# Scores of a windowed attention in 64x64 tiles, each query half with the 192 keys that it may see

## The chip, the cores and the metric

The kernel runs on one core of a Trainium2 chip. The metric is the device time of one execution in microseconds (us). TensorE (PE in the profile) multiplies, PEld is the loading of its stationary operand, VectorE (DVE), ScalarE (ACT) and GpSimd (POOL) do the rest, and SyncE (SP) issues the DMAs.

## The reference

The model is an adaLN block on `x` of 2 x 2048 x 256 in float32. Its first half is three layers of causal linear attention with a feed-forward part; its second half is two layers of windowed attention, 8 heads of 64, window 128, with a gated feed-forward part. The change touches the scores of the second half alone:

```python
def local_attention(q, k, v):
    b, h, n, d = q.shape
    w = n // WINDOW
    bq = q.reshape(b, h, w, WINDOW, d) * QK_SCALE
    bk = k.reshape(b, h, w, WINDOW, d)
    ...
    bk, bv = (look_around(bk), look_around(bv))   # block before and own block
    sim = jnp.einsum('bhwid,bhwjd->bhwij', bq, bk)
    mask = (i < j) | (i > j + WINDOW) | (j == -1)
    sim = jnp.where(mask, -jnp.finfo(sim.dtype).max, sim)
    attn = jax.nn.softmax(sim, axis=-1)
```

A query at place r of its block sees the keys r to 127 of the block before and the keys 0 to r of its own: 129 of 256. Of the 256 columns of a score row, queries 0 to 63 never need the last 64, and queries 64 to 127 never the first 64.

## The kernel before

The second half works on 64 units of 128 tokens (2 layers, 2 batch rows, 16 blocks each); unit u is a block, and units with u % 16 == 0 have no block before them. The heads stand as four head pairs: in `QT` and `KT` the 128 partitions are two heads of 64 features, and a head pair's 128 tokens are 128 columns. `KT` keeps two units' keys, the present one in slot u % 2 and the one before in the other slot, so that in odd units the block before comes first in it, and in even ones the present block.

The order of every engine's work is written out by hand: a long list of calls such as `scores_tile(u, hf)`, `turn_weights(u, g)`, `mix(u, hf)`, with semaphores (`e.wait_ge(*...at(u))`, `.then_inc(...)`) between engines. Within that list, feed-forward work of other tokens (`up`, `gate`, `down` in fp32r as three products of high and low parts) is laid between the steps of attention.

For each unit and each half `hf` of the head pairs: `scores_tile` writes the scores of two head pairs into PSUM banks 3 and 4 (`PS[:, 3 + par, ...]`, one bank for each head of the pair); DVE `largest` adds the mask `MSK` and takes row maxima over the PSUM tile, in place; ACT `exps` writes `PR`; PE `turn_weights` transposes `PR` back into PSUM; `copy_p` (half on ACT, half on DVE) writes `PT`; PE `mix` multiplies with the values `VV`. ACT's `copy_k` (line 2206) and `copy_q` (line 2213) fill `KT` and `QT` after PE has transposed keys and queries (lines 927 and 936). Products with plain fp32 operands appear in the trace as two weight loads and two matmul records each (two passes), fp32r products and transposes as one.

In `scores_tile` the stationary operand is `QT[r, c]`, 64 features by 128 queries, the moving one is `KT[r, :, c]`, 256 keys as two pieces of 128. The two heads of a pair stand in different partition halves and go to different row halves of the array. All matmuls are recorded under the helper `mm` at line 276; `PS<-KT,QT` names the scores, `PS<-PT,VV` the products with the values.

Of the kernel before, what the change touches and what calls it, by code (L numbers as in the profile page):

```python
# [41 lines left out]
def build(nc, ctx, ins, out):  # L42
# [252 lines left out]
    def wt(nm, a, n):  # L295
        o = REG[nm] + a
        if nm == "w1":
            return W1H[:, o:o + n], W1L[:, o:o + n]
        if nm == "w2":
            return W2H[:, o:o + n], W2L[:, o:o + n]  # L300
        return WQH[:, o:o + n], WQL[:, o:o + n]

    def va(o, n):
# [116 lines left out]
    def _(e):  # L420
# [518 lines left out]
        def scores_tile(u, hf):  # L939
            if not 0 <= u < NU:  # L940
                return
            first, cur = u % 16 == 0, u % 2
            e.wait_ge(*b_qt.at(u))
            e.wait_ge(*b_kt.at(u))
            if hf:
                e.wait_ge(*b_pt[0].at(u))
                e.wait_ge(*g_pt[0].at(u))
            elif u >= 1:
                e.wait_ge(*b_rs.at(u - 1))
                e.wait_ge(*g_pt[1].at(u - 1))  # L950
            else:
                e.wait_ge(*d_h.at(23, 1))
                e.wait_ge(*g_x.at(2))
            for i in range(2):
                for par in range(2):
                    r, c = slice(64 * par, 64 * par + 64), slice(128 * (2 * hf + i), 128 * (2 * hf + i) + 128)
                    if first:
                        m = mm(e, PS[:, 3 + par, 256 * i + 128 * cur:256 * i + 128 * cur + 128], QT[r, c], KT[r, cur, c], i == 0)
                    else:
                        m = mm(e, PS[:, 3 + par, 256 * i:256 * i + 256].rearrange("p (b n) -> p b n", b=2), QT[r, c], KT[r, :, c], i == 0)  # L960
            m.then_inc(*f_sc[hf].up(u))

        def blocks(u):
            return (u % 2,) if u % 16 == 0 else (0, 1)

# [11 lines left out]
        def mix(u, hf):  # L977
# [10 lines left out]
            for i in range(2):  # L988
                hp = 2 * hf + i
                for b in blocks(u):  # L990
                    for par in range(2):
                        start = hf == 0 and i == 0 and b == blocks(u)[0]
                        v = u if b == u % 2 else u - 1
                        m = mm(e, PS[64 * par:64 * par + 64, 2, 128 * hp:128 * hp + 128], VV[:, v % 3, 64 * (2 * hp + par):64 * (2 * hp + par) + 64],
# [877 lines left out]
    def _(e):  # L1872
# [328 lines left out]
        def copy_k(u):  # L2201
            if 0 <= u < NU:
                e.wait_ge(*f_tk.at(u))
                if u >= 1:
                    e.wait_ge(*f_sc[1].at(u - 1))
                e.copy(KT[:, u % 2, :], PS[:, 7, :]).then_inc(*b_kt.up(u))

# [7 lines left out]
        def exps(u, g):  # L2215
            if not 0 <= u < NU:
                return
            hf, par, S = g // 2, g % 2, SM[:, u % 4, :]
            lo, hi = (128 * (u % 2), 128 * (u % 2) + 128) if u % 16 == 0 else (0, 256)
            e.wait_ge(*g_bi[g].at(u))  # L2220
# [10 lines left out]
        def copy_p(u, hf):  # L2231
            if not 0 <= u < NU:
                return
            lo, hi = (128 * (u % 2), 128 * (u % 2) + 128) if u % 16 == 0 else (0, 256)
            e.wait_ge(*f_wg[2 * hf].at(u))
# [739 lines left out]
    def _(e):  # L2975
# [580 lines left out]
        def largest(u, g):  # L3556
            if not 0 <= u < NU:
                return
            hf, par, S = g // 2, g % 2, SM[:, u % 4, :]
            lo, hi = (128 * (u % 2), 128 * (u % 2) + 128) if u % 16 == 0 else (0, 256)  # L3560
            z = 128 if u % 16 == 0 else (0 if u % 2 else 128)
            if u == 0:
                e.wait_ge(*t_ms.at())
            e.wait_ge(*f_sc[hf].at(u))
            for i in range(2):
                o = PS[:, 3 + par, 256 * i + lo:256 * i + hi]
                t = e.tensor_tensor_reduce(o, o, MSK[:, z:z + hi - lo], 1.0, NEG, ALU.add, ALU.max, S[:, 32 + 2 * g + i:33 + 2 * g + i])  # L3567
            t.then_inc(*g_tt[g].up(u))
# [5 lines left out]
        def copy_p(u, hf):  # L3574
            if not 0 <= u < NU:
                return
            lo, hi = (128 * (u % 2), 128 * (u % 2) + 128) if u % 16 == 0 else (0, 256)
            e.wait_ge(*f_wg[2 * hf + 1].at(u))
# [1957 lines left out]
```

## Time and profile before

| | |
|---|---|
| time, median of 3 runs | 2609.28 us (2607.87 to 2610.86) |
| profiled execution | 2610.22 us, its span 2608.4 us |
| busy in the span | PE 97%, DVE 82%, POOL 55%, ACT 54% |
| chain that ended last | PE 87%, DVE 6%, issue 3%, ACT 2%, POOL 1% |
| mean granted TensorE clock | 0.989 of full speed |
| scores of the second half | 128 calls, 1024 matmul records, 142.8 us busy |

The 1.8 us between the span and the execution's time lie around the program. Busy time of PE is the union of its records; since the ends of matmuls are modelled and overlap their successors, what a group costs is read from its start to the start of the next group.

### The profile page before, as it was taken

What the parts mean: (1) busy time and instruction counts of PE and PEld (TensorE: products, weight loads), DVE (VectorE), ACT (ScalarE), POOL (GpSimd) and SP (SyncE); (2) the same over time, 40 slices, a digit from 0 to 9 for tenths busy, and PEclk for the clock granted to TensorE, in tenths of its full rate; (3) what the DMA queues carried; (4) which work ended last, traced back from release to release, by engine and by line L of the source; (5) the groups of instructions that cost most, each with busy time, mean ns of one, the idle gap of its engine ahead of it and who ended that gap; (6) DMA issues with size and microseconds to landing.
All of it is one profiled execution on the core that took longest, in us unless ns stands there. A gap on an engine that the chain in (4) does not pass through costs nothing.

```text
span 2608.4 us, 65564 instructions
## 1 busy us (share of the span) xinstructions
PE 2523.3 (97%) x23520; PEld 2094.4 (80%) x23520; DVE 2143.9 (82%) x5253; ACT 1405.0 (54%) x2945; POOL 1427.1 (55%) x1406
## 2 busy tenths in 40 slices
PE   6899999999999999999998999999999999999998
PEld 4688888888888888887776788888888888888877
DVE  5798888887787788898999887888898887888875
ACT  3343344334433443344256777777776777777761
POOL 2253444443444355455576666666676766776664
PEclk8899999999999999999999999999999999999999
DMA  3100000010000010000112000000111100110001
GB/s 91 38 18 10 18 2 18 14 36 2 2 2 14 14 42 10 18 26 26 49 38 66 21 17 19 12 16 17 32 32 36 33 29 23 32 32 28 27 29 49
DMA packets 79088, 67.44 MB, mean 26 GB/s; under 512 B 15896, under 2 KB 73368, under 8 KB 78776
## 3 DMA queue, kind: packets, MB, share of 16 engines
q1 hardware_dynamic: 78776, 63.25, 8.1%
q8 instruction: 199, 3.26, 0.5%
q14 instruction: 113, 0.93, 0.1%
HBM read 49.18 MB, written 12.58 MB: 24 GB/s over the span
## 4 chain that ended last, share of the span: by engine, by line
PE 87%; DVE 6%; issue 3%; ACT 2%; POOL 1%; DMA 0%; SPq 0%; DVEq 0%; ACTq 0%; POOLq 0%
PE PS L276 76%; PE PS L974 4%; PE PS L936 1%; PE PS L1004 1%; PE PS L927 1%; PE PS L488 1%; PE PS L498 1%; PE PS L431 1%; PE PS L885 1%; DVE U L3159 1%; DVE PS L3567 1%; PE PS L1034 1%; DVE Z L2997 0%; ACT PR L2227 0%; DVE X L3005 0%
## 5 line engine op out<-in xcount | busy, mean ns | idle before, releaser
L2227 ACT ACTIVATE PR<-PS,SM 128x256 f32<-128x256 f32 (+1 forms) x512 | 280.7, 561 | 136.5 <-DVE SM L3572 135.9
L1913 ACT ACTIVATE FB<-PS,BC 128x512 f32<-128x512 f32 x192 | 133.5, 695 | 322.1 <-PE PS L276 174.9
L3159 DVE TENSOR_TENSOR U<-PS,CST 128x512 f32<-128x512 f32 x384 | 238.0, 681 | 37.5 <-PE PS L276 37.4
L4597 POOL TENSOR_TENSOR RL<-FB,RH 128x512 fp32r<-128x512 f32 x96 | 125.7, 1310 | 219.6 <-DVE RH L3136 219.6
L4819 POOL TENSOR_TENSOR SM<-SM,COL 128x8 f32<-128x8 f32 x128 | 224.6, 1755 | 10.7
L276 PE MATMUL PS<-W2H,RH 128*128 128x256 f32 x768 | 226.1, 294 | 2.2 <-POOL RL L4597 2.2
L3567 DVE CUSTOM_DVE_ANT_0 PS<-PS,MSK 128x256 f32<-128x256 f32 (+1 forms) x512 | 202.5, 436 | 30.5 <-PE PS L276 29.5
L276 PE MATMUL PS<-W2H,RL 128*128 128x256 f32 x768 | 215.8, 281 | 0.0
L276 PE MATMUL PS<-W2L,RH 128*128 128x256 f32 x768 | 215.7, 281 | 0.0
L4609 POOL TENSOR_TENSOR SBD<-SBD,TMP 128x256 f32<-128x256 f32 x84 | 64.8, 772 | 197.0 <-DVE TMP L3151 197.0
L276 PEld LDWEIGHTS PS<-W2H,RH 128*128 128x128 f32 x768 | 145.0, 189 | 25.0 <-issue 20.4
L276 PE MATMUL PS<-X1H,W1H 128*128 128x512 f32 x384 | 160.9, 419 | 3.5 <-ACT FB L1913 2.4
L276 PE MATMUL PS<-VAH,XBH 128*128 128x512 f32 x384 | 162.9, 424 | 1.0 <-ACT SQ L2176 0.6
L276 PE MATMUL PS<-X1L,W1H 128*128 128x512 f32 x384 | 151.7, 395 | 0.0
L276 PE MATMUL PS<-VAH,XBL 128*128 128x512 f32 x384 | 151.3, 394 | 0.0
L276 PE MATMUL PS<-VAL,XBH 128*128 128x512 f32 x384 | 151.2, 394 | 0.0
L276 PE MATMUL PS<-X1H,W1L 128*128 128x512 f32 x384 | 151.0, 393 | 0.0
L276 PE MATMUL PS<-KT,QT 64*128 64x256 f32 (+1 forms) x1024 | 142.8, 397 | 8.4 <-ACT PT L2240 5.8
L276 PEld LDWEIGHTS PS<-W2L,RH 128*128 128x128 f32 x768 | 145.2, 189 | 2.4
L276 PEld LDWEIGHTS PS<-W2H,RL 128*128 128x128 f32 x768 | 145.1, 189 | 0.0
L974 PE MATMUL PS<-CST,PR 128*128 128x128 f32 x992 | 137.4, 274 | 7.7 <-ACT PR L2227 7.6
L4832 POOL TENSOR_TENSOR OTL<-OO,OTH 128x512 fp32r<-128x512 f32 x64 | 83.0, 1296 | 103.8 <-ACT OTH L2263 103.6
(268 smaller groups left out, 8467.4 us busy)
## 6 DMA issues: line engine op xcount, KB each, us to landing
PX<-in_L_attn_x SPq DMA_DIRECT2D x16, 512.0 KB, 3.9
TB<-in_k_rot SPq DMA_DIRECT2D x64, 128.0 KB, 2.1
SG<-in_L_attn_W SPq DMA_DIRECT2D x24, 256.0 KB, 2.8
xp_scratch<-PX SPq DMA_DIRECT2D x8, 512.0 KB, 2.9
xs_scratch<-X SPq DMA_DIRECT2D x64, 64.0 KB, 1.5
ZS<-xs_scratch SPq DMA_DIRECT2D x16, 256.0 KB, 2.8
GG<-xp_scratch SPq DMA_DIRECT2D x7, 512.0 KB, 3.7
out<-GG SPq DMA_DIRECT2D x7, 512.0 KB, 2.9
```

The source lines that it names most:

```text
L276: return e.matmul(o, l, r, start=start, stop=True, skip_group_check=True)
L431: t = e.transpose(PS[:, 2 + k, 128 * j:128 * j + 128], X[:, 4 * c + j, 128 * k:128 * k + 128], IDN)
L488: t = e.transpose(PS[:, i, D * j + 128 * m:D * j + 128 * m + 128], FK[:, m, 128 * (2 * i + j):128 * (2 * i + j) + 128], IDN)
L974: m = e.transpose(PS[:, 3 + par, a:a + 128], PR[:, par, a:a + 128], IDN)
L1913: e.activation(FB[:, hb % 2, :], PS[:, 5, :], ACT.Relu, bias=BC[:, l % 2, 4 + hb:5 + hb]).then_inc(*a_re.up(n, hb))
L2227: t = e.activation(PR[:, par, 256 * i + lo:256 * i + hi], PS[:, 3 + par, 256 * i + lo:256 * i + hi], ACT.Exp, bias=S[:, 40 + 2 * g + i:41 ...
L3159: e.tensor_tensor(heads(U[:, u % 6, :], 4), heads(PS[:, g, :], 4), bcast(CM, 4), ALU.mult).then_inc(*d_mk.up(n, u))
L3567: t = e.tensor_tensor_reduce(o, o, MSK[:, z:z + hi - lo], 1.0, NEG, ALU.add, ALU.max, S[:, 32 + 2 * g + i:33 + 2 * g + i])
L4597: e.tensor_tensor(RL[:, r, :], FB[:, 0, :], RH[:, r, :].bitcast(F), ALU.subtract).then_inc(*p_rl.up(n, hb))
L4609: e.tensor_tensor(SBD[:, (tile + 1) % 2, :, :], SBD[:, tile % 2, :, :], TMP[:, :, :], ALU.add).then_inc(*p_sd.up(n, j))
L4819: e.tensor_tensor(o, a, MHALF.broadcast_to([128, 8]), ALU.pow).then_inc(*h_rs[i].up(u))
L4832: e.tensor_tensor(OTL[:, :], OO[:, :], OTH[:, :].bitcast(F), ALU.subtract).then_inc(*h_ol.up(u))
```

## The change

Each head of a head pair's scores is cut into two query halves. The stationary operand is now 64 features by 64 queries, and the four combinations of head and query half use four quarters of the array: rows by head, columns by query half. The first query half gets the keys 0 to 191 of the sequence (block before, own block), the second the keys 64 to 255. In PSUM the block before now always stands first. `KT` is laid out anew: for each head pair slot 0 and slot 1 stand beside each other, so that the 192 keys are contiguous where slot 0 holds the block before (odd units). In even units the two pieces stand in the wrong order for that, and each tile takes two matmuls of 128 and 64 or of 64 and 128 keys. A call of `scores_tile` thus issues 4 matmuls of 256 columns before; now 8 of 192 columns in the 32 odd units, 16 of 64 or 128 columns in 28 even units, and in the 4 first units of a row 8 of 64 or 128 columns where there were 4 of 128. The 64 columns that a query half does not write keep what PSUM held, and the mask puts them out.

```diff
+    def keys_of(b):
+        return KT.rearrange("p x (h b n) -> p (x h) b n", h=2, b=2)[:, :, b, :]
...
             for i in range(2):
+                c = 128 * (2 * hf + i)
                 for par in range(2):
-                    r, c = slice(64 * par, 64 * par + 64), slice(128 * (2 * hf + i), 128 * (2 * hf + i) + 128)
-                    if first:
-                        m = mm(e, PS[:, 3 + par, 256 * i + 128 * cur:256 * i + 128 * cur + 128], QT[r, c], KT[r, cur, c], i == 0)
-                    else:
-                        m = mm(e, PS[:, 3 + par, 256 * i:256 * i + 256].rearrange("p (b n) -> p b n", b=2), QT[r, c], KT[r, :, c], i == 0)
+                    for half in range(2):
+                        r, p, a = slice(64 * par, 64 * par + 64), slice(64 * half, 64 * half + 64), 256 * i
+                        Q = QT[r, c + 64 * half:c + 64 * half + 64]
+                        if first or cur == 0:
+                            before, here = 128 if half == 0 else 64, 64 if half == 0 else 128
+                            if not first:
+                                mm(e, PS[p, 3 + par, a + 128 - before:a + 128], Q, keys_of(1 - cur)[r, 2 * hf + i, 128 - before:128], i == 0)
+                            m = mm(e, PS[p, 3 + par, a + 128:a + 128 + here], Q, keys_of(cur)[r, 2 * hf + i, 0:here], i == 0 and first)
+                        else:
+                            m = mm(e, PS[p, 3 + par, a + 64 * half:a + 64 * half + 192], Q, KT[r, hf, 256 * i + 64 * half:256 * i + 64 * half + 192], i == 0)
             m.then_inc(*f_sc[hf].up(u))

         def blocks(u):
-            return (u % 2,) if u % 16 == 0 else (0, 1)
+            return (1,) if u % 16 == 0 else (0, 1)
...
-                        v = u if b == u % 2 else u - 1
+                        v = u - 1 + b
...
-                e.copy(KT[:, u % 2, :], PS[:, 7, :]).then_inc(*b_kt.up(u))
+                e.copy(keys_of(u % 2), PS[:, 7, :].rearrange("p (h n) -> p h n", h=4)).then_inc(*b_kt.up(u))
...
-            z = 128 if u % 16 == 0 else (0 if u % 2 else 128)
...
-                t = e.tensor_tensor_reduce(o, o, MSK[:, z:z + hi - lo], 1.0, NEG, ALU.add, ALU.max, S[:, 32 + 2 * g + i:33 + 2 * g + i])
+                t = e.tensor_tensor_reduce(o, o, MSK[:, lo:hi], 1.0, NEG, ALU.add, ALU.max, S[:, 32 + 2 * g + i:33 + 2 * g + i])
```

`exps`, `copy_p` and `largest` use `lo, hi = 128 if u % 16 == 0 else 0, 256`; their sizes stay.

PE, an odd unit in the second half, scores between projections and a product of the feed-forward part. Before (a row is line, operation, output and operands, shape of the output, how many in a row):

```order
L276 MATMUL PS<-VAH,XBH 128x512
L276 MATMUL PS<-VAL,XBH 128x512
L276 MATMUL PS<-VAH,XBL 128x512
L276 MATMUL PS<-KT,QT 128x256 x4
L276 MATMUL PS<-VBH,RH 128x256 x4
```

After, the same place:

```order
L276 MATMUL PS<-VAH,XBH 128x512
L276 MATMUL PS<-VAL,XBH 128x512
L276 MATMUL PS<-VAH,XBL 128x512
L276 MATMUL PS<-KT,QT 64x192 x8
L276 MATMUL PS<-VBH,RH 128x256 x4
```

Four matmuls have become eight narrower ones, and nothing around them has moved.

PE, an even unit that is not the first of its row, scores between the products with the values and transposes of the feed-forward part. Before:

```order
L1004 MATMUL PS<-CST,RX 128x128 x4
L276 MATMUL PS<-PT,VV 64x128 x8
L276 MATMUL PS<-KT,QT 128x256 x4
L1034 MATMUL PS<-CST,ZS 128x128 x8
L885 MATMUL PS<-CST,X 128x128 x2
```

After:

```order
L1013 MATMUL PS<-CST,RX 128x128 x4
L276 MATMUL PS<-PT,VV 64x128 x8
L276 MATMUL PS<-KT,QT 64x128
L276 MATMUL PS<-KT,QT 64x64 x2
L276 MATMUL PS<-KT,QT 64x128 x2
L276 MATMUL PS<-KT,QT 64x64 x2
L276 MATMUL PS<-KT,QT 64x128 x2
L276 MATMUL PS<-KT,QT 64x64 x2
L276 MATMUL PS<-KT,QT 64x128 x2
L276 MATMUL PS<-KT,QT 64x64 x2
L276 MATMUL PS<-KT,QT 64x128
L1043 MATMUL PS<-CST,ZS 128x128 x8
```

Here four matmuls have become sixteen, and two that follow each other go to the same quarter of the array: 128 and 64 columns to the first, 64 and 128 to the second, and so on.

## Rows read from the trace of the kernel before

**Rows 1.** The page: busy us, share of the span, number of instructions.

```profile
PE 2523.3 (97%) x23520; PEld 2094.4 (80%) x23520; DVE 2143.9 (82%) x5253; ACT 1405.0 (54%) x2945; POOL 1427.1 (55%) x1406
```

**Rows 2.** Busy time by stretch: us, busy (instructions), PEclk, DMA share, GB/s.

```profile
1306.00:1400.00 94.00, 83.96 (x585) 67.48 (x583) 90.98 (x254) 52.19 (x130) 68.20 (x68) 0.98 0.19 53
1400.00:2500.00 1100.00, 1087.50 (x7941) 903.76 (x7942) 910.95 (x2592) 812.35 (x1857) 741.34 (x762) 1.00 0.09 27
2500.00:2608.00 108.00, 93.89 (x628) 79.78 (x626) 68.93 (x161) 37.72 (x83) 48.69 (x43) 0.95 0.12 37
```

**Rows 3.** Waits of PE, 1306 to 2608 us: total, times, longest.

```profile
PE PS L974 <- ACT PR L2227: 7.6, 12, 1.6
PE PS L276 <- ACT PT L2240: 5.8, 7, 0.9
...
PE PS L276 <- DVE PT L3583: 2.5, 3, 1.3
```

**Rows 4.** PE's groups: busy us, mean ns, idle before.

```profile
L276 PE MATMUL PS<-KT,QT 64*128 64x256 f32 x960 | 137.1, 404 | 7.6 <-ACT PT L2240 5.1 <-DVE PT L3583 2.5
...
L276 PE MATMUL PS<-KT,QT 64*128 64x128 f32 x64 | 5.7, 297 | 0.7 <-ACT PT L2240 0.7
```

**Rows 5.** PE's timeline in two units: start us, length us, instruction, number.

```profile
1956.93 1.13 PE L276 MATMUL PS<-KT,QT 64*128 64x256 f32 x8
1957.99 1.09 PE L276 MATMUL PS<-PT,VV 128*64 128x128 f32 x16
1959.02 0.66 PE L936 MATMUL PS<-CST,QS 128*128 128x128 f32 x4
...
1618.97 0.71 PE L276 MATMUL PS<-KT,QT 64*128 64x128 f32 x8
1619.61 0.66 PE L1034 MATMUL PS<-CST,ZS 128*128 128x128 f32 x4
```

**Rows 6.** The same scores cut off at 1957.20 and at 1957.40 us.

```profile
1956.93 0.49 PE L276 MATMUL PS<-KT,QT 64*128 64x256 f32 x2
...
1956.93 0.70 PE L276 MATMUL PS<-KT,QT 64*128 64x256 f32 x4
```

**Rows 7.** Weight loads (PEld), 1306 to 2608 us: busy us, mean ns, idle before.

```profile
L276 PEld LDWEIGHTS PS<-PT,VV 128*64 128x64 f32 x1984 | 107.5, 138 | 31.9 <-issue 31.3
L276 PEld LDWEIGHTS PS<-KT,QT 64*128 64x128 f32 x1024 | 88.1, 187 | 40.2 <-issue 31.8
```

**Rows 8.** PE's timeline in the first half, four column groups.

```profile
928.51 0.33 PE L276 MATMUL PS<-VP,KS 128*32 128x32 f32 x16
928.65 1.06 PE L276 MATMUL PS<-U,VP 128*32 128x128 f32 x32
929.64 1.15 PE L276 MATMUL PS<-FQ,FK 32*128 32x256 f32 x16
```

**Rows 9.** PE's timeline in the first half, sixteen 32x32 tiles, two passes each.

```profile
914.23 0.62 PE L276 MATMUL PS<-U,OM 32*32 32x512 f32 x3
914.25 0.61 PE L276 MATMUL PS<-KS,OM 32*32 32x512 f32 x1
...
914.33 0.61 PE L276 MATMUL PS<-KS,OM 32*32 32x512 f32 x1
914.68 0.60 PE L276 MATMUL PS<-U,OM 32*32 32x512 f32 x3
...
915.11 0.82 PE L276 MATMUL PS<-U,CST 32*32 32x512 f32 x3
```

**Rows 10.** Groups of ACT and DVE, 1306 to 2608 us: busy us, mean ns, idle before.

```profile
L2240 ACT COPY PT<-PS 128x512 f32<-128x512 f32 x120 | 70.3, 586 | 39.7 <-PE PS L974 39.2
...
L2206 ACT COPY KT<-PS 128x512 f32<-128x512 f32 x64 | 37.5, 586 | 43.3 <-PE PS L927 41.5 <-PE PS L276 1.8
...
L3567 DVE CUSTOM_DVE_ANT_0 PS<-PS,MSK 128x256 f32<-128x256 f32 x480 | 193.8, 444 | 29.2 <-PE PS L276 28.4
```

More of the change, by code:

```diff
@@ L2218, in exps @@
             hf, par, S = g // 2, g % 2, SM[:, u % 4, :]
-            lo, hi = (128 * (u % 2), 128 * (u % 2) + 128) if u % 16 == 0 else (0, 256)
+            lo, hi = 128 if u % 16 == 0 else 0, 256
             e.wait_ge(*g_bi[g].at(u))
@@ L2233, in copy_p @@
                 return
-            lo, hi = (128 * (u % 2), 128 * (u % 2) + 128) if u % 16 == 0 else (0, 256)
+            lo, hi = 128 if u % 16 == 0 else 0, 256
             e.wait_ge(*f_wg[2 * hf].at(u))
@@ L3559, in largest @@
             hf, par, S = g // 2, g % 2, SM[:, u % 4, :]
-            lo, hi = (128 * (u % 2), 128 * (u % 2) + 128) if u % 16 == 0 else (0, 256)
-            z = 128 if u % 16 == 0 else (0 if u % 2 else 128)
+            lo, hi = 128 if u % 16 == 0 else 0, 256
             if u == 0:
@@ L3576, in copy_p @@
                 return
-            lo, hi = (128 * (u % 2), 128 * (u % 2) + 128) if u % 16 == 0 else (0, 256)
+            lo, hi = 128 if u % 16 == 0 else 0, 256
             e.wait_ge(*f_wg[2 * hf + 1].at(u))
```

## The prediction

> **What bounds the kernel now.** I read the busy shares first: PE is busy 97% of the span, every other engine less [rows 1]. Then the second half by stretch, since the change lies only there: from 1400 to 2500 us PE is busy 1087.5 of 1100 us at the full clock, with DVE at 83%, ACT at 74% and POOL at 67%; in the first 94 us DVE is the fuller one (91 of 94), and the last 108 us are an emptying tail [rows 2]. Third the waits: PE's longest kinds of wait in the half are 7.6 us behind the exponentials and 5.8 and 2.5 us behind the copies of the weights [rows 3]. So between 1400 and 2500 us the time is what PE's list of matmuls costs, and a microsecond taken from it is nearly a microsecond of the kernel. The scores are 1024 matmul records, of which 960 have 256 columns [rows 4]; what they cost has to be read from start to start.
>
> **How such a matmul is priced.** A call of `scores_tile` with 256 columns takes 1957.99 − 1956.93 = 1.06 us, one with 128 columns 1619.61 − 1618.97 = 0.64 us [rows 5]. Each is eight records, but two run at a time: 0.27 us after the start only two are on record, at 1957.40 four [rows 6]. So it is four turns of two, and 128 more columns cost 0.42/4 = 0.105 us a turn, or 0.82 ns a column. What remains is fixed: 0.64 − 0.42 = 0.22 us for the first weights, which nothing hides, and for running empty before the array is set up for another shape. A load of 64 stationary columns is recorded 49 ns shorter than one of 128 (138 against 187 ns) [rows 7]; the products with the values fit that, eight turns of 128 columns in 1.03 us, 0.19 us of it fixed [rows 5].
>
> **Do four quarters run at once?** The scores before use two row halves, the products with the values two column halves, and no row shows both together at 64x64. The nearest rows do more: with sixteen 32x32 tiles all first passes start between 914.23 and 914.33 us and the second ones from 914.68, 0.45 us later for 512 columns at a price of 0.42 [rows 9], so rows and columns combine at full rate, about 7 ns from one start to the next. With four column groups over the same rows, 16 passes of 32 columns, each with weights of its own, take 928.65 − 928.51 = 0.14 us, 0.035 a turn of four, where streaming alone is 0.026 [rows 8]. So weights for one column group load while another works, and a turn costs some 5 to 9 ns beyond its columns. The Trainium skill says otherwise ("TensorE: Matmul & The Clock Gate", Part 3, The mechanism): weight loads overlap running matmuls only where the row groups differ. By it each call would show four loads more, some 0.2 us, and most of the gain would go; the rows on four column groups contradict it.
>
> **Odd units (32 units, 64 calls).** Eight matmuls of 192 columns on four quarters are again four turns, of 192 columns: 0.64 + 4 × 64 × 0.82 ns = 0.85, less 0.05 for the shorter first weights, plus two more starts of 7 ns: 0.81 us for 1.06. 64 × 0.25 = 16.0 us. This has one answer.
>
> **First units (4 units, 8 calls).** 64 and 128 columns on the two halves: the 128 set the time, as before, with shorter first weights. 0.64 to 0.60 us, 8 × 0.04 = 0.3 us.
>
> **Even units (28 units, 56 calls).** This is the disputed part. Sixteen matmuls; each quarter gets 128 + 64 or 64 + 128 columns a head pair, 192 again, but in eight passes instead of four. If the quarters work independently, the call is an odd unit's plus four passes a quarter at 5 to 9 ns: 0.81 + 0.03 = 0.84 us, and 56 × 0.22 = 12.3 us are saved. But now two successive matmuls go to the same quarter, and if the second has to wait at the head of the queue, the other quarters behind it starve. No row of before shows two successive matmuls for one quarter with matmuls for others behind them; all its tiled groups change the tile with every matmul. For independence speaks that a later matmul does pass an earlier one's second pass: the second head's first pass is on record 0.3 us before the first head's second one [rows 6], and sixteen matmuls are open at once, each with its second pass to come, when the next starts [rows 9]. The queue is therefore no strict line of passes. Whether it is a strict line of matmuls it doesn't say. I take independence, since whatever holds back sixteen second passes has room for one matmul that waits for its quarter; the other end is priced as a rival.
>
> **The rest.** ACT's copy into `KT` now writes four pieces of 128 at a stride; it is 586 ns now, the same as the copy into `PT` [rows 10]; nothing in its size changes and I cost it at nothing. If it grew by 0.1 us, 64 × 0.1 us on an engine at 74% would hide under PE. DVE's `largest` and the exponentials keep their shapes [rows 10]; the unwritten 64 columns are read as before. No wait and no DMA is added, and no queue is passed.
>
> **Sum.** 16.0 + 0.3 + 12.3 = 28.6 us less on PE. Not all arrives: the first 94 us, where DVE is fuller than PE, and the tail hold about 200 of 1302 us, so roughly a tenth of the calls, and what waits there are stays. I take 2 us off: 26.6. Against the profiled execution (2610.2 us) that is 2583.6, against the median of the runs (2609.3, 0.9 lower) 2582.7, say 2583. If the other engines followed worse than that, 5 us more would be lost; if the even calls cost as little as the odd ones, 1.7 us would be won: this case alone holds 2576 to 2591.
>
> **Rivals.**
> 1. *The waiting matmul blocks the queue until its quarter can take its weights* (0.18, slower). Per head pair the four quarters then begin one after the other, each new one only when the one before has begun its second pass: load 0.05 + first pass 0.107, load 0.05 + 0.055, and the same again, 0.52 to 0.57 us with the starts. Two head pairs 1.14, then the last quarter's last 0.055 + 2 × 0.107, and 0.09 to run empty: 1.5 us for 1.06. 56 × 0.44 = 24.6 us lost against 16.3 won: 2617. It decides on the even units alone: beyond 1.35 us a call the change loses.
> 2. *Matmuls start strictly in program order* (0.13, slower). Then the second matmul of a quarter starts only after the first has ended, and the next quarter with it: 0.218 + 0.11 + 0.218 + 0.11 = 0.66 us a head pair, twice, plus 0.218 at the end and 0.14 fixed, 1.67 us a call; 56 × 0.61 = 34 lost, net 18 slower: 2627. The rows neither show nor exclude it. This is also a rule of the Trainium skill, in the place named above: matmuls start and end in program order, a strict FIFO.
> 3. *PE gets ahead and then waits for others* (0.10, of which 0.08 faster and 0.02 the same). After the scores come mask and maxima on DVE (444 ns each, four a call) [rows 10] and the exponentials before PE may transpose. The work between stays the same, so the distance is kept, and PE's waits of that kind are only 16 us [rows 3]; against it speaks too that DVE has 17% free. If half of the gain went so: 2596.
> 4. *The four quarters don't overlap* (0.02, slower): two at a time, eight turns of 192 columns, 1.4 us a call and 2650; the rows on sixteen tiles speak against it.
>
> **How the numbers follow.** Forecast 0.57, rivals 0.18, 0.13, 0.10, 0.02. Faster by over 0.2% (5 us, about what a measurement of this kernel can tell from no change): 0.57 + 0.08 = 0.65; same 0.02; slower 0.33. The cases lie on both sides. The likeliest one's own range is 2576 to 2591; to hold 8 in 10 the range has to reach over rival 3 and most of rival 1: 2576 to 2622, which leaves out rivals 2 and 4 and edges.
>
> **What would show it.** Per call, start to next start: odd 0.81 us (all cases but rival 4), first 0.60, even 0.84 (forecast), 1.5 (rival 1), 1.67 (rival 2). In an even call cut off 0.1 us after its start, four matmuls should be under way; under rivals 1 and 2 it is one or two. The waits of PE behind `PR` and `PT` should stay near 16 us; under rival 3 they grow by 10 or more. I am wrong outright if the odd calls don't shrink by 0.25 us, or if ACT's copy into `KT` grows enough to be waited for.

## The result, and the profile after

Four runs of each kernel give a median of 2594.05 us after (2589.8 to 2596.7) for 2608.66 us before: a ratio of 0.9941 with an interval of 0.9924 to 0.9958. In a second series, of five rounds, it was 2589.34 for 2605.40 us, 0.9936 (0.9924 to 0.9949). By the medians the change takes 14.6 and 16.1 us off; the forecast was 26.6. The sign and the range hold, and more than ten microseconds of the forecast are missing. One execution of a kernel below (rotated, `turn_tile` and `high_x` later) took 8366 us, for a reason that no trace shows, and is left out of its median.

The page of after (answers to [rows 1]; chain by engine; groups as on the page):

```profile
PE 2499.2 (97%) x25440; PEld 2085.6 (81%) x25440; DVE 2147.5 (83%) x5253; ACT 1404.7 (54%) x2945; POOL 1428.8 (55%) x1406
...
PE 86%; DVE 7%; issue 4%; ACT 2%; POOL 1%; DMA 1%; SPq 0%; DVEq 0%; ACTq 0%; POOLq 0%
```

The same stretches as in [rows 2] (length, PE, PEld, DVE, ACT, POOL busy, granted clock, DMA share, GB/s):

```profile
1306.00:1400.00 94.00, 81.63 (x729) 66.85 (x727) 89.81 (x265) 54.63 (x140) 69.03 (x72) 0.97 0.21 58
1400.00:2500.00 1100.00, 1086.08 (x9806) 913.65 (x9808) 926.62 (x2613) 820.60 (x1874) 749.01 (x769) 1.00 0.09 26
2500.00:2588.00 88.00, 72.51 (x503) 61.84 (x497) 51.97 (x116) 24.73 (x52) 35.37 (x28) 0.95 0.14 45
```

PE is as full as before, with the clock at its full level between 1400 and 2500 us; DVE goes from 911 to 927 us in the middle stretch, because the same work now stands in less time. The waits of PE in the second half are those of [rows 3], nearly unchanged:

```profile
PE PS L276 <- ACT PT L2249: 6.7, 8, 1.0
PE PS L983 <- ACT PR L2236: 6.6, 12, 1.5
...
PE PS L276 <- DVE PT L3591: 1.5, 2, 1.3
...
PE PS L888 <- DVE OO L3610: 0.9, 4, 0.3
```

One kind is new, the last: L888 is `turn_tile`, the transposes of `X` (line 885 before), and `OO` is what DVE makes of the products with the values. It looks like nothing, 0.9 us in four places. It will turn out to be most of what is missing. ACT's copy into `KT` and DVE's maxima have kept their lengths [rows 10]; only the idle time ahead of the maxima has shrunk from 29.2 to 13.7 us:

```profile
L2215 ACT COPY KT<-PS 128x512 f32<-128x512 f32 x63 | 36.9, 586 | 37.9 <-PE PS L930 36.4 <-PE PS L276 1.5
...
L3575 DVE CUSTOM_DVE_ANT_0 PS<-PS,MSK 128x256 f32<-128x256 f32 x480 | 193.7, 444 | 13.7 <-PE PS L276 10.9
```

Now the calls themselves, on PE's timeline of after: a first unit's, an even unit's and an odd unit's, each with the group that follows [rows 5]. A group bears the name of the form it begins with, so the 32 records of the even call are those of 128 and of 64 columns.

```profile
1608.85 0.67 PE L276 MATMUL PS<-KT,QT 64*64 64x64 f32 x16
1609.45 0.33 PE L1043 MATMUL PS<-CST,ZS 128*128 128x128 f32 x1
...
1960.40 0.96 PE L276 MATMUL PS<-KT,QT 64*64 64x128 f32 x32
1961.30 0.33 PE L276 MATMUL PS<-PT,VV 128*64 128x128 f32 x2
...
1979.29 0.88 PE L276 MATMUL PS<-KT,QT 64*64 64x192 f32 x16
1980.10 0.39 PE L276 MATMUL PS<-VBH,RH 128*128 128x256 f32 x1
```

The odd call takes 0.81 us, as forecast; the first one 0.60, as forecast; the even one 0.90 us (0.895 in the median), where 0.84 was forecast. The records inside the even call say which picture of the queue is right. Windows that begin with the call and look at the scores alone (length, PE busy, records, clock, DMA):

```profile
1960.40:1960.45 0.05, 0.04 (x4) 1.00 0.00 0
1960.40:1960.60 0.20, 0.20 (x9) 1.00 0.00 0
```

Within 0.05 us four matmuls are under way, the first ones of the four quarters, 13 to 14 ns apart. The trace gives their lengths as 128, 64, 128 and 64 columns, where the program's first four are 128, 64, 64 and 128: these are matmuls 1, 3, 5 and 7. Each but the first stands in the program behind the second matmul of the quarter before, which has to wait; they have passed it. That refutes rivals 1 and 2 for this order.

**A better measure than the span.** The kernel's first half, which no edit touches, varies between executions: the first scores of the second half start at 1308.7 us in the profiled run of before, at 1301.8 in that of after, and between 1300.6 and 1308.7 in all fourteen profiled runs, those of the experiments included. Of the 20.4 us between the two spans, 7 lie ahead of the first changed instruction. I therefore read each trace from the first scores of unit 4 to the first scores of unit 62. Two executions of before give 1116.6 and 1116.9 us for this stretch of 58 units, two of after 1103.6 and 1103.6. The change is worth 13.1 us there; by the forecast it should be 58 × 0.25 + 6 × 0.04 + 52 × 0.22 = 26.2.

Where the 13.1 us are, by what PE issues, each group from its start to the next start: scores −18.1, transposes of `X` in `turn_tile` +2.3, transposes of `PR` +0.8, products with the values +0.5, all else +1.4.

### The profile page after: what moved, and what is told of

Same layout as the page of the kernel before. It is cut to its first block, busy times and chain, and to the rows that moved or that the text cites. A ratio compares the mean times of both kernels' runs of the same rounds, so it can differ in the third digit from the quotient of the medians.

```text
span 2588.0 us, 69404 instructions
## 1 busy us (share of the span) xinstructions
PE 2499.2 (97%) x25440; PEld 2085.6 (81%) x25440; DVE 2147.5 (83%) x5253; ACT 1404.7 (54%) x2945; POOL 1428.8 (55%) x1406
## 4 chain that ended last, share of the span: by engine, by line
PE 86%; DVE 7%; issue 4%; ACT 2%; POOL 1%; DMA 1%; SPq 0%; DVEq 0%; ACTq 0%; POOLq 0%
PE PS L276 75%; PE PS L983 4%; PE PS L939 1%; PE PS L930 1%; PE PS L1013 1%; PE PS L501 1%; PE PS L491 1%; PE PS L434 1%; PE PS L888 1%; PE PS L1043 1%; DVE U L3168 0%; DVE PS L3575 0%; DVE Z L3006 0%; DVE ST L2995 0%; DVE X L3014 0%
## 5 line engine op out<-in xcount | busy, mean ns | idle before, releaser
L276 PE MATMUL PS<-HTH,VBH 128*128 128x512 f32 x330 | 138.6, 420 | 1.0 <-ACT G L2301 0.8
L276 PE MATMUL PS<-PT,VV 128*64 128x128 f32 x1984 | 139.1, 282 | 0.6 <-DVE XBL L3535 0.6
```

Source lines behind the costliest of these rows:

```text
L276: return e.matmul(o, l, r, start=start, stop=True, skip_group_check=True)
```

## The experiments

A ratio is to before in the same series, on the same chip, with its 95% interval; the series ran on three chips, with medians of before between 2605.4 and 2607.0 us, so the ratios are to be compared, not the medians. "The stretch" is units 4 to 61 as just defined, from one trace of each kernel; "against before" is its difference from 1116.6 us.

| kernel | median us | ratio | stretch us | against before |
|---|---|---|---|---|
| before (second execution) | 2602.3, one run | | 1116.9 | +0.3 |
| the change, again | 2589.3 | 0.9936 (0.9924 to 0.9949) | 1103.6 | −13.0 |
| quarters in odd units alone | 2598.7 | 0.9969 (0.9955 to 0.9982) | 1110.3 | −6.3 |
| rotated quarters | 2584.2 | 0.9919 (0.9906 to 0.9932) | 1100.6 | −16.0 |
| one quarter's matmuls in a row | 2646.4 | 1.0151 (1.0136 to 1.0166) | 1155.9 | +39.2 |
| three key slots | 2592.0 | 0.9950 (0.9938 to 0.9962) | 1105.1 | −11.6 |
| `turn_tile` later | 2597.6 | 0.9968 (0.9956 to 0.9980) | 1114.8 | −1.8 |
| rotated, `turn_tile` and `high_x` later | 2586.2 | 0.9931 (0.9918 to 0.9944) | 1102.0 | −14.7 |
| three slots, the same two later | 2590.9 | 0.9946 (0.9934 to 0.9958) | 1104.7 | −11.9 |
| before with a short `OO` | 2599.3 | 0.9973 (0.9961 to 0.9984) | 1112.7 | −4.0 |
| the change with a short `OO` | 2574.9 | 0.9882 (0.9865 to 0.9898) | 1089.8 | −26.8 |
| rotated, `reduce` behind the maxima | 2583.1 | 0.9911 (0.9898 to 0.9925) | 1100.7 | −15.9 |

### The change and the kernel before, once more

> The changed kernel once more, for a second profile and more times. The first profile showed odd calls of 0.81 us, even ones of 0.895, first ones of 0.598, and the transposes behind 45 of the calls (turn_tile, on PSUM bank 2) starting 0.955 us after the scores' start whatever the scores took, behind DVE's product OO. Theory 1 (the price list of PE less that new floor): 16.1 + 9.5 + 0.4 us saved on calls, 5.2 us given back at the floor, so 20.8 us below the kernel before: 2588 in the median, and the floor at 0.955 again. Theory 2 (something varies from run to run and takes more in most runs): the median stays near 2594, and a profile of such a run shows waits that the first one did not have.

> The kernel before once more, for a second profile. In the profiles so far the first scores start between 1300.6 and 1308.7 us, though nothing ahead of them differs. Theory 1 (the first half varies from execution to execution, and only the distance from the first scores to the end may be compared between profiles): the first scores may start anywhere from 1300 to 1309 us, and from there to the end it is 1299.7 us again, within 2. Theory 2 (the change speeds up the first half too, by where its instructions lie): the first scores start near 1308.7 us again.

They repeat the stretch to 0.3 us and the ratio to 0.0005, while the first scores start 6.5 us apart in the two of before and 4.3 in the two of after. Both pairs suggest that differences of a microsecond in the stretch can be trusted; in the span they can't. The calls and the 0.955 us are those of the first profile, but the 20.8 us that theory 1 worked out from them are not reached: 16.1 by the medians. From the first scores to the end before takes 1298.3 us for 1299.7, as its theory 1 had it.

### Quarters in the odd units alone

```diff
                     if first:
...
+                        m = mm(e, PS[:, 3 + par, a + 128 * cur:a + 128 * cur + 128], QT[r, c:c + 128], keys_of(cur)[r, 2 * hf + i, :], i == 0)
+                    elif cur == 0:
+                        m = mm(e, PS[:, 3 + par, a:a + 256], QT[r, c:c + 128], KT[r, hf, a:a + 256], i == 0)
                     else:
...
+                        for half in range(2):
+                            m = mm(e, PS[64 * half:64 * half + 64, 3 + par, a + 64 * half:a + 64 * half + 192], QT[r, c + 64 * half:c + 64 * half + 64],
+                                   KT[r, hf, a + 64 * half:a + 64 * half + 192], i == 0)
```

> The kernel before with quarters in the odd units alone; even and first units keep 64x128 tiles and all their keys, with the keys laid out anew. Theory 1 (the prices add): 64 odd calls of 0.81 instead of 1.064 save 16.1 us, of which 29 calls in front of turn_tile give 0.144 each back, so 12 us below the kernel before, 2597, and the even units' part of the change is worth the other 8.5. Theory 2 (the list is not what binds): odd alone already gives all of the 14.6 us that the medians show.

The calls are 0.811 us in odd and 1.065 in even units, so a call's price doesn't depend on the other units' form. But 58 odd calls at −0.254 us are 14.7, and the stretch gives 6.3; the scores themselves show only −9.25. Theory 1 had 12 us for the kernel, theory 2 all of 14.6; the medians give 6.7, and neither holds. More than half of what the odd calls save doesn't arrive. So the loss is not a matter of the even units' sixteen matmuls.

### The second matmul of a quarter moved behind the other quarters

```diff
+                for piece in range(2 if cur == 0 and not first else 1):
+                    for par in range(2):
+                        for half in range(2):
...
+                            elif cur == 0 and piece == half:
+                                m = mm(e, PS[p, 3 + par, a + 128 - before:a + 128], Q, keys_of(1 - cur)[r, 2 * hf + i, 128 - before:128], i == 0 and piece == 0)
+                            elif cur == 0:
+                                m = mm(e, PS[p, 3 + par, a + 128:a + 128 + here], Q, keys_of(cur)[r, 2 * hf + i, 0:here], i == 0 and piece == 0)
```

In even units every head pair now issues its 128 columns on all four quarters and then its 64 on all four.

> The changed kernel with the even units' sixteen matmuls in another order: the four quarters in turn, first all pieces of 128 keys, then all of 64, so that no two successive matmuls go to the same quarter. Theory 1 (two successive matmuls for one quarter cost the 0.055 us that an even call has above my 0.84): even calls fall from 0.895 to 0.84 us; those 16 in front of turn_tile win nothing because of the floor at 0.955, the other 40 win 0.055 each, 2.2 us less than the changed kernel. Theory 2 (the passes of 64 columns cost it, in any order): even calls stay at 0.89 and the time too. If a queue of whole matmuls had been blocked in the changed kernel, its even calls would have been 1.5 us, which the profile already excludes.

The same even call in this kernel:

```profile
1959.57 0.90 PE L276 MATMUL PS<-KT,QT 64*64 64x128 f32 x32
1960.40 0.33 PE L276 MATMUL PS<-PT,VV 128*64 128x128 f32 x2
```

0.83 us (0.828 in the median) for 0.895, with the same matmuls; the first four start 7 ns apart instead of 13, and the turns of the four quarters stay in step, where in the change two quarters begin with 64 columns and two with 128 and their turns fall out of step. Fourteen of the stretch's 52 even calls are held at 0.955 us in both kernels, for a reason given below, and win nothing; the other 38 × 0.067 make 2.5 us. The scores alone show 2.3, the stretch 3.0 and the medians 5.2. This is the forecast's 0.84, found in another order of the same instructions. How much of the 0.067 us comes from the passing and how much from the uneven turns, this run doesn't tell apart.

### All matmuls of one quarter behind each other

```diff
-            for i in range(2):
-                c = 128 * (2 * hf + i)
-                for par in range(2):
-                    for half in range(2):
+            for par in range(2):
+                for half in range(2):
+                    for i in range(2):
+                        c = 128 * (2 * hf + i)
```

Odd units then have two matmuls for a quarter in a row, even ones four.

> The changed kernel with the same matmuls in the worst order for a queue: all those of one quarter of the array behind each other (two in odd units, four in even ones), then the next quarter's. Theory 1 (each quarter takes its own matmuls out of the queue, whatever stands in front for another quarter): odd calls stay near 0.81, at most 0.87, even ones near 0.90 and below 1.0. Theory 2 (at most one matmul per quarter may be passed by others, which the changed kernel's order never exceeded): odd calls near 0.85, but even ones above 1.3, since the third matmul for a quarter holds up the other three quarters.

Even call, and windows from its start on (scores alone):

```profile
1993.72 2.05 PE L276 MATMUL PS<-KT,QT 64*64 64x128 f32 x32
1995.70 0.33 PE L276 MATMUL PS<-PT,VV 128*64 128x128 f32 x2
```

```profile
1993.72:1993.77 0.05, 0.05 (x1) 1.00 0.00 0
1993.72:1994.10 0.38, 0.38 (x4) 1.00 0.00 0
1993.72:1994.13 0.41, 0.41 (x6) 1.00 0.00 0
```

The odd call takes only 0.83 us for 0.81: the second matmul of a quarter waits, and the other quarters pass it. The even call takes 1.98 us, more than either rival had for the change. At first one record is under way where the change has four; for 0.38 us only four passes start, those of the first quarter's first two matmuls. Then, at 0.384 us, its third starts, and 5 ns later (0.389) the second quarter's first. That is what a queue would do that holds back one waiting matmul for each quarter and stops at the next: the third could step aside only when the second had started, the fourth only when the third had. Of the first eight matmuls of a call in the change one waits for each quarter, four in all, and none of them stops another. That the queue is built so is inferred from the starts in these two orders; no row shows it directly. I had taken "whatever holds back sixteen second passes has room for one matmul that waits"; it has, and for one only.

The Trainium skill says of this ("TensorE: Matmul & The Clock Gate", Part 3, The mechanism) that matmuls keep program order at both ends, a strict FIFO. The windows of the change contradict it: four records within 0.05 us, of matmuls 1, 3, 5 and 7 of the call. What an order that stops the queue costs is this run's: 52 even calls × 1.085 us are 56.4 more than the change, and the stretch is 52.3 longer.

### Three key slots, so that even units too take 192 columns at once

`KT` gets a third slot, block before, own, and a second copy of the even units' keys, made by ACT; the even units then issue the odd ones' eight matmuls. Room for it comes from letting `RX` be `RS`, so that ACT's copy into `RX` now waits for `OO` too (the last line).

```diff
-                            if not first:
-                                mm(e, PS[p, 3 + par, a + 128 - before:a + 128], Q, keys_of(1 - cur)[r, 2 * hf + i, 128 - before:128], i == 0)
-                            m = mm(e, PS[p, 3 + par, a + 128:a + 128 + here], Q, keys_of(cur)[r, 2 * hf + i, 0:here], i == 0 and first)
...
+                            m = mm(e, PS[p, 3 + par, a + 64 * half:a + 64 * half + 192], Q, key_row(2 * hf + i)[r, z:z + 192], i == 0)
...
+        def twin_k(u):
+            if 0 <= u < NU and u % 2 == 0:
+                e.wait_ge(*b_kt.at(u))
+                e.copy(keys_of(0), keys_of(2)).then_inc(*b_kd.up(u))
...
+                    e.wait_ge(*g_om.at(u - 1))
```

> The changed kernel with a third slot of keys: an even unit's keys go to slot 2, behind the odd unit's in slot 1, and ACT copies them once more into slot 0 for the next unit (64 partitions' pairs as before, 128x512, ahead of the first exponentials); so even units too issue eight matmuls of 192 keys. To make room, the sums' two buffers became one. Theory 1 (an even call then costs what an odd one does, 0.81): 40 calls win 0.084 each over the changed kernel, 3.4 us, the 16 in front of turn_tile nothing, and ACT's 32 further copies of 0.59 us hide in its waits for DVE; about 2586 where the changed kernel is 2589. Theory 2 (the copies delay the exponentials): PE waits more for PR and the time is like the changed kernel's or above it.

The even call falls to 0.811 us, and the kernel is no faster than the change: stretch 1105.1 for 1103.6. The scores are 3.0 us shorter than in the change, the transposes of `PR` 2.6 us longer: ACT has a copy more ahead of the exponentials, and PE waits a little longer for those, 2.9 us in the stretch for 1.9. The waits of the second half, 7.6 us for 6.6 in the change:

```profile
PE PS L989 <- ACT PR L2247: 7.6, 14, 1.5
```

How much of the loss comes from the copies and how much from the shared buffer and its wait, this run doesn't tell apart. Against the rotated order, which needs no copy, there is nothing to gain here.

### Who holds the first half's calls

Of the two calls of a unit only the second (`hf` 1) shows its full gain. The first is followed by `turn_tile`, and there the gain is cut. PE and DVE in before, first call of an odd unit:

```profile
1984.39 1.13 PE L276 MATMUL PS<-KT,QT 64*128 64x256 f32 x8
1984.48 0.69 DVE L3602 TENSOR_TENSOR OO<-PS,RS 128x512 f32<-128x512 f32 x1 [1.62 <-PE PS L276]
...
1985.45 0.44 PE L885 MATMUL PS<-CST,X 128*128 128x128 f32 x2
...
1985.66 0.47 PE L276 MATMUL PS<-VAH,XBH 128*128 128x512 f32 x1
```

The same place in after:

```profile
1969.87 0.88 PE L276 MATMUL PS<-KT,QT 64*64 64x192 f32 x16
1969.99 0.69 DVE L3610 TENSOR_TENSOR OO<-PS,RS 128x512 f32<-128x512 f32 x1 [1.56 <-PE PS L276]
...
1970.83 0.41 PE L888 MATMUL PS<-CST,X 128*128 128x128 f32 x2
...
1971.17 0.47 PE L276 MATMUL PS<-VAH,XBH 128*128 128x512 f32 x1
```

`turn_tile` writes into PSUM bank 2, where the products with the values stand, and first waits until DVE has read them for `OO` (`g_om`, line 884 of after). `OO` starts about 0.1 us after the scores, when the products with the values have ended, and takes 0.69 us. In after it ends at 1970.68, and the transposes start 0.15 us later, at 1970.83: 0.955 us after the scores, which themselves could have given way after 0.811. In before the same wait would have let them go after 0.955 us as well, and the scores took 1.065: a margin of 0.11 us, of which the tables of waits show nothing, and a saving of 0.25 us used it up. In 37 of the 42 first calls of the stretch that `turn_tile` follows, the transposes start 0.95 to 0.96 us after the scores, whether the scores cost 0.811 or 0.895; in before it is 1.065. (Sixteen of its 58 first calls have something else behind them; ten of these are even units' and show their 0.895.) With a few longer ones that makes 5.7 us, 23.8 at the calls' own prices less the 18.1 read.

The trace also has the sequencer's own records. It passes the wait for `OO` at 1970.72, 0.11 us before the transposes, and the three waits behind it at 1970.85, 1970.96 and 1971.06. In before the same four pass at 1985.21, .34, .44 and .55, and the transposes start 0.24 us after the first. Over all 60 places that distance is 0.22 us in the median in before and 0.107 in after. So the next group starts 0.34 us after the transposes where it was 0.21 (medians of the 42: 0.34 and 0.23), since the waits behind `OO`'s are worked off one by one, some 0.11 us each; that makes the 2.3 us on the transposes. The profile puts 0.9 us down to `OO`, since it counts gaps between PE's records, and the modelled ends leave almost none.

Two kinds of experiment test that: another order on PE, and a shorter `OO`.

### `turn_tile` one entry later

```diff
             scores_tile(u + 1, 0)
+            partner(q, 1)
             turn_tile(u + 4)
-            partner(q, 1)
```

and so in every unit where something can stand between.

> The changed kernel with turn_tile put one entry later in PE's list, behind the projection, output product or feed-forward product that followed it, wherever it stood right behind the first scores of a unit. Theory 1 (the transposes wait for PSUM bank 2, that is for DVE's product OO, and this ate 5.2 us of the gain): PE finds the bank free, all odd calls take 0.81 and even ones 0.895 us to the next start, and the kernel is about 5 us below the changed one. Theory 2 (the tiles' copies on ACT come later and hold back the exponentials behind them): PE waits more for PR, and the time is the same or 2 to 5 us longer.

Both calls now show 0.811 and 0.895 us, and the scores save 23.1 us instead of 18.1, as theory 1 says. And the kernel gets slower than the change, by 11.3 us in the stretch, more than either theory had: the transposes of `PR`, counted to the start of the next group, cost 16.0 us more than before, and other products some 5. PE's waits in units 4 to 61 of this kernel:

```profile
PE PS L276 <- ACT GG L2301: 8.1, 11, 0.7
PE PS L983 <- ACT PR L2236: 4.6, 7, 2.1
```

and the second of these kinds in the change, where the first isn't among the waits:

```profile
PE PS L983 <- ACT PR L2236: 1.9, 4, 0.7
```

ACT takes `X` out of PSUM (`high_x`) ahead of the exponentials and, in one unit of four, of `gelu`, which writes `GG`, in a fixed order. A later `turn_tile` makes ACT wait, the exponentials start later (3.71 us after the scores on the average, for 3.49), and `gelu` behind them too. Most of the 16.0 us is PE's wait not for the exponentials but for `gelu`: 11.5 of them lie where a product of the feed-forward part follows the transposes, and eleven of these stand 0.7 us each behind `GG`. The edit took one wait away and made a greater one two steps on, rival 3's kind of mechanism, but from my own edit.

### Rotated, with `turn_tile` and `high_x` later

```diff
             scores_tile(u + 1, 0)
+            partner(q, 1)
             turn_tile(u + 4)
-            partner(q, 1)
...
-        high_x(8)
         high_o(4)
         exps(5, 1)
         copy_v(6)
         exps(5, 0)
+        high_x(8)
```

> The kernel with rotated quarters, with turn_tile one entry later in PE's list, and besides with ACT's copy of the turned tile (high_x) behind the first two exponentials instead of in front of them. With turn_tile alone moved, PE found bank 2 free but waited 16 us more for the exponentials. Theory 1 (those waits came from ACT standing in front of high_x while PE was late with the tile): PE's waits for PR fall back, the scores cost 0.81 and 0.83 us everywhere, and the kernel is 5 to 8 us below the one with rotated quarters alone, some 2578 against 2584. Theory 2 (the tile itself comes too late, for the projections that read it): PE waits in front of the projections instead and the time is no better than with rotated quarters alone.

> Three slots of keys together with turn_tile one entry later and ACT's high_x behind the first two exponentials. Theory 1 (the gains add): all calls 0.81 us, no wait behind OO, about 2 us below the kernel with rotated quarters and those two moves. Theory 2 (ACT, now with 32 copies more and its order changed, comes late): PE's waits for PR and PT rise and the time is above that kernel's.

The expectation says that PE waited 16 us more for the exponentials; as just shown, most of that was for `gelu`. With `high_x` behind the first two exponentials, the scores show their whole gain (−26.2 us), and the surplus on `PR` falls from 16.0 to 7.5 us: the waits for `GG` are gone, so that half of it was indeed ACT's order. It is still no better than rotation alone (1102.0 for 1100.6 us), and with three slots likewise 1104.7. PE's waits behind `PR`, in units 4 to 61, have grown threefold against the change:

```profile
PE PS L986 <- ACT PR L2239: 5.7, 16, 1.5
```

The time is what theory 2 had, but the waits are for `PR` and not in front of the projections. What is taken from one wait is found at the next; that the chain scores, maxima, exponentials, transposes has no slack left in these units is my reading of it, which these runs don't prove.

### A short `OO` in both kernels

```diff
-            e.tensor_tensor(OO[:, :], PS[:, 2, :], RS[:, :], ALU.mult).then_inc(*g_om.up(u))
+            w = 512 if u == 0 else 64
+            e.tensor_tensor(OO[:, 0:w], PS[:, 2, 0:w], RS[:, 0:w], ALU.mult).then_inc(*g_om.up(u))
```

From unit 1 on both kernels leave out seven eighths of this product, 0.23 us on DVE instead of 0.69. All else is issued as before, so the pair measures the change with `OO` off the path.

> The kernel before with the product OO cut to 64 of its 512 columns after the first unit (the output is then not the reference's), so that DVE's 0.69 us between the products with the values and the masks becomes about 0.15. It is the partner of the changed kernel with the same cut. In the kernel before PE hardly waits for DVE there, so both theories expect little: the same, or up to 5 us faster.

> The changed kernel with the product OO cut to 64 of its 512 columns after the first unit (the output is then not the reference's). Theory 1 (the gain that is missing is held by OO: the transposes of turn_tile wait for it, and PE's sequencer stands in front of that wait instead of working off the next ones): the transposes start 0.81 and 0.895 us after the scores, and this kernel lies 22 to 26 us below the kernel before with the same cut, where the full kernels lie 15 to 17 apart. Theory 2 (OO is only where PE happens to wait; the chain through masks and exponentials is what holds): the difference stays at 15 to 18 us and the waits move to the exponentials PR.

The change with a short `OO`, first call of an odd unit:

```profile
1963.02 0.88 PE L276 MATMUL PS<-KT,QT 64*64 64x192 f32 x16
1963.14 0.23 DVE L3611 TENSOR_TENSOR OO<-PS,RS 128x64 f32<-128x64 f32 x1 [1.58 <-PE PS L276]
...
1963.83 0.44 PE L888 MATMUL PS<-CST,X 128*128 128x128 f32 x2
...
1964.02 0.48 PE L276 MATMUL PS<-VAH,XBH 128*128 128x512 f32 x1
```

The transposes follow after 0.81 us and the next group 0.19 us after them. Between the two kernels with a short `OO` the stretch differs by 22.9 us, the medians by 24.4; 23.8 would be the calls at their measured prices (58 × 0.254 + 52 × 0.169 + 6 × 0.047), and the scores alone show 23.3. So with `OO` out of the way nearly everything arrives, and 22.9 − 13.1 = 9.8 us is what `OO` costs the change beyond what it costs before: 7.5 at `turn_tile` itself (5.2 on the scores, 2.3 on the transposes), 1.5 on the transposes of `PR`, the rest elsewhere. A short `OO` also frees 0.46 us of DVE a unit, and the last 2.3 us may be DVE's load as a whole and not the wait. Before gains 4.0 us by the same cut, and 4.2 lie on the transposes of `X`: there too some of what `OO` holds up was lost behind it, and the change lost more.

### DVE's `reduce` moved behind the maxima

```diff
-            reduce(u + 3, 0)
             largest(u + 2, 1)
             largest(u + 2, 0)
+            reduce(u + 3, 0)
```

> The kernel with rotated quarters and, on DVE, the sum of squares (reduce) that stood between OO and the masks moved behind the masks, where it did stand there (7 places by hand and two in the loop over four units). Theory 1 (DVE between OO and the masks sets when the exponentials of the first head pairs can start, so that faster scores don't bring them forward): masks start 0.2 to 0.3 us earlier on average in those calls, and the kernel is 2 to 4 us below the one with rotated quarters. Theory 2 (the sums of squares are as urgent, since the keys' rotation and the transposes for the next unit wait for them): the same or slower.

In the first calls the maxima now start 1.02 us after the scores on the average and the exponentials 3.19, where they start at 1.18 and 3.48 us in the rotated kernel, and the stretch doesn't move (1100.7 for 1100.6): PE's transposes of `PR` stand 6.0 us behind the scores in both. Theory 1's 2 to 4 us don't come. The ratio of 0.9911 is the lowest of all full kernels and within the interval of the rotated one's 0.9919.

## Why the prediction was right in sign and ten microseconds off

- **What bounds the kernel.** Right: with `OO` short, 22.9 of 23.8 us taken off PE's list arrive. The list of waits was read with gaps: between the kinds it names stand 4.5 us of issue and one wait of 3.2 us for a DMA into `VBH`, longer than the 2.5 it has as third; that one is 3.5 us in after and explains nothing here.
- **Four quarters at once, odd units.** Right: 0.81 us. The argument from the rows on sixteen tiles and four column groups [rows 8, 9] held. Rival 4 is out.
- **First units.** Right: 0.60 us.
- **Even units.** The quarters do work independently, as long as one matmul waits for each. The term was mis-sized: 0.895 us for 0.84, which is 52 × 0.055 = 2.9 us of the stretch. The step that failed is "plus four passes a quarter at 5 to 9 ns", which takes the turns of the quarters to be in step; rotated, they are, and 0.828 results.
- **Rivals 1 and 2.** Refuted for the order of the change by matmuls 1, 3, 5 and 7 within 0.05 us. Blocking exists, however, one matmul later than rival 1 had it: where a quarter has two waiting, an even call costs 1.98 us.
- **"Not all arrives", 2 us.** This step failed, and it carries most of the error. I took the work outside 1400 to 2500 us for the only place where something else is late, and read PE's waits [rows 3] as the list of what could become late. A wait that is over 0.11 us before it would hold anything is in no such list. `turn_tile` directly behind the scores, waiting for `OO`, was there in the order and in the timeline; the saving of 0.25 or 0.17 us was greater than that margin, and 37 of the stretch's 110 odd and even calls stop at 0.955 us. Measured: 9.8 us in the stretch, and 0.9 more that didn't arrive even with `OO` short.
- **Rival 3.** The time is nearer to its 2596 us than to the forecast's 2583, and its kind of mechanism, PE ahead and waiting, did come, with some 10 us for the 13.3 that it was priced at. But the place was wrong: not the exponentials behind the scores, whose wait stayed at 6.6 us [rows 3 has 7.6], but DVE's `OO` of the step before. Its sign, waits behind `PR` and `PT` grown by 10 us, did not show: they are 14.8 us for 15.9.
- **The range.** The forecast's own case was given 2576 to 2591 us; the first median, 2594.1, is above it, the second, 2589.3, inside. That both lie in 2576 to 2622 is owed to the room made for rivals 1 and 3, not to the sum.
- **ACT's copy, DVE's maxima, queues.** Right at nothing: 586 and 444 ns as before.

The sum as it should have been, for the stretch: 23.8 for the calls, less 9.8 behind `OO`, makes 14.0; 13.1 were measured. The 9.8 are themselves a difference of measured stretches, so this divides the loss up and doesn't test it; the 0.9 between is what is missing with a short `OO` as well. Outside the stretch there was nearly nothing to win: from the first scores to the end of the span the change saves 13.5 us in the profiled runs, 0.4 more than the stretch. What the medians show beyond that, 14.6 and 16.1 us, is no more than the first half varies by.

**A version that beats both.** The rotated order, 0.9919 of before and 3.0 us less than the change in the stretch, with no other edit. The intervals of the two ratios overlap (0.9906 to 0.9932, and 0.9924 to 0.9949), so it rests on the stretch, and on the shorter call that explains 2.3 of the 3.0 us. What still lies in the first calls, some 8 us, needs `OO` out of `turn_tile`'s way, for example another PSUM bank for the products or an earlier `OO`; that wasn't tried.

## What to carry to other kernels

Before a shortened group is priced, look at what the instruction behind it waits for, and by how much that wait is over before; that margin, not the table of waits, says how much of the saving arrives. With tiles of the array in use, issue matmuls so that the quarter changes with each and all quarters get equal lengths in turn; one waiting matmul a quarter was passed at a small cost here, a second one brought everything to a stop. Where a first part that isn't touched varies by 8 us, compare traces between two marks inside the part that is.

## What the runs showed of the hardware that I had not expected

- A matmul that waits for its quarter of the array was passed by later ones for other quarters (1, 3, 5 and 7 of a call within 0.04 us), so the starts aren't in program order. With four for one quarter behind each other the next quarter started only with the first one's third matmul, at 0.39 us, and the same 16 matmuls took 1.98 us for 0.895.
- The same sixteen matmuls cost 0.828 us in step and 0.895 out of step.
- PE's sequencer passed the waits that stand behind each other at about 0.11 us each, in before as in after. Where the first of them was held by `OO`, the next group came 0.34 us after the transposes instead of 0.19 to 0.23.
- The unchanged first half took between 1300.6 and 1308.7 us, while the stretch of 58 units repeated within 0.3 us.
